# In every slot, TensorE projects the values' columns before it transposes the attention's outputs, instead of after

## The reference

```
q, k, v = split(shift_tokens(x) @ Wqkv[i])           # 16 heads of 64
q, k    = rotary(l2norm(q) * q_scale), rotary(l2norm(k) * k_scale)
sim     = q @ k_window.T * 8, masked                  # windows of 32 tokens, each looks at itself and the one before
x       = softmax(sim) @ v_window  merged @ Wo + x
a, gate = split(layernorm(shift_tokens(x)) @ W1 + b1)
x       = a * gelu(gate) @ W2 + b2 + x
```

## Time and profile before

| | |
|---|---|
| time, median of 3 runs | 4077.79 us (4077.22 to 4078.13) |
| the profiled execution: its own time | 4067.75 us |
| its span, first to last instruction | 4066.0 us |
| granted TensorE clock, mean over the span | 0.964 of 2.4 GHz |
| PE busy | 3616.5 us, 89% of the span |
| weight loads (overlap PE) | 2665.1 us, 66% |
| DVE busy | 2853.2 us, 70% |
| ACT busy | 2465.4 us, 61% |
| POOL busy | 1858.0 us, 46% |

### The profile page before, as it was taken

How to read it: one execution, slowest core, us unless ns; L and a number is a source line. 1 busy time by engine, 2 the same in 40 slices (tenths; PEclk the granted TensorE clock), 3 DMA queues, 4 the chain that set the end, 5 groups by cost and what they waited for, 6 DMA issues and landing times. The chain is left out here.

```text
span 4066.0 us, 155656 instructions
## 1 busy us (share of the span) xinstructions
PE 3616.5 (89%) x66756; PEld 2665.1 (66%) x66756; DVE 2853.2 (70%) x4768; ACT 2465.4 (61%) x4661; POOL 1858.0 (46%) x1559
## 2 busy tenths in 40 slices
PE   4996998998999998999998999998999998999995
PEld 3884666666666666666666666666666666666663
DVE  3116777778777778777778777777777777777773
ACT  2224666667666666666666666666666666666664
POOL 2003554455545555555545544544544545445441
PEclk9667999999999999999999999999999999999998
DMA  2211101111101011110111100111100111101002
GB/s 51 41 20 48 34 27 29 32 44 39 32 27 33 28 49 36 30 32 27 33 44 36 34 28 27 33 44 36 34 28 27 33 44 36 34 28 32 28 28 73
DMA packets 163065, 142.00 MB, mean 35 GB/s; under 512 B 87097, under 2 KB 112464, under 8 KB 161616
## 3 DMA queue, kind: packets, MB, share of 16 engines
q1 hardware_dynamic: 155866, 132.04, 11.9%
q10 hardware_dynamic: 6518, 0.03, 0.1%
HBM read 28.35 MB, written 6.36 MB: 9 GB/s over the span
## 5 line engine op out<-in xcount | busy, mean ns | idle before, releaser
L1094 POOL TENSOR_TENSOR nat<-ra,rb 128x512 f32<-128x512 f32 x768 | 1003.0, 1306 | 1154.4 <-DVE ra L1149 1137.8
L1098 POOL TENSOR_TENSOR nat<-nat,rr 128x512 f32<-128x512 f32 x768 | 820.1, 1068 | 675.8 <-ACT rr L1048 620.7
L1148 DVE TENSOR_TENSOR rb<-ps,tab 128x512 f32<-128x512 f32 x768 | 526.3, 685 | 342.8 <-ACT sq L988 340.1
L785 PE MATMUL ps<-wh,xls 128*128 128x512 f32 x1152 | 613.9, 533 | 29.7 <-PEq L132 29.6
L988 ACT ACTIVATE sq<-ps 128x512 f32<-128x512 f32 x768 | 449.4, 598 | 190.6 <-PE ps L787 146.9
L820 PE MATMUL ps<-kT,qT 64*32 64x64 f32 x24704 | 450.4, 220 | 94.3 <-issue 91.6
L1149 DVE TENSOR_TENSOR ra<-ps,tab 128x512 f32<-128x512 f32 x768 | 522.4, 680 | 0.0
L820 PEld LDWEIGHTS ps<-kT,qT 64*32 64x32 f32 x24704 | 372.0, 106 | 193.0 <-issue 177.4
L801 PE MATMUL ps<-con,nat 128*128 128x128 f32 x3080 | 425.7, 274 | 47.7 <-POOL nat L1098 37.7
L1180 DVE TENSOR_REDUCE nrm<-sq 128x16 f32<-128x1024 f32 x384 | 463.8, 1208 | 0.0
L786 PE MATMUL ps<-wl,xhs 128*128 128x512 f32 x1152 | 458.5, 398 | 0.0
(11 more groups left out here) (165 smaller groups left out, 5710.1 us busy)
## 6 DMA issues: line engine op xcount, KB each, us to landing
v<-v SPq DMA_DIRECT2D x192, 396.0 KB, 3.6
v<-v SPq DMA_DIRECT2D x96, 132.0 KB, 3.5
raw<-in_L_ffn_Wqkv SPq DMA_DIRECT2D x6, 1536.0 KB, 6.5
v<-v SPq DMA_DIRECT2D x96, 66.0 KB, 3.2
vbd<-vD SPq DMA_DIRECT2D x128, 32.2 KB
wo<-in_L_ffn_Wo SPq DMA_DIRECT2D x6, 512.0 KB, 5.2
xnat<-in_L_attn_hidden_states SPq DMA_DIRECT2D x8, 256.0 KB, 3.5
vD<-vs SPq DMA_DIRECT2D x8, 256.0 KB, 2.3
```

Source lines behind the costliest of these rows:

```text
L785: nc.tensor.matmul(dst, al, bh, start=True, stop=False)
L1094: nc.gpsimd.tensor_tensor(nat[:, k, :], ra[:, k, :], rb[:, k, :], ALU.add).then_inc(cur["add"], 1)
L1098: nc.gpsimd.tensor_tensor(nk, nk, rr[:, k, :].unsqueeze(2).broadcast_to([P, 8, DH]), ALU.mult).then_inc(cur["qkn"], 1)
L1148: nc.vector.tensor_tensor(heads8(rb[:, k, :]), heads8(ps[:, bank, :])[:, :, ::-1, :], sin, ALU.mult)
```

## The change

In PE's list of a slot, the wait for `ke` and `project(i, 2, TT)` move from behind the previous row's piece to between `scores` and `turn_out`. Nothing is added or removed, and the lists of the other engines are the same.

```diff
@@ def tensor(pe), the loop over the slots
                     scores(i)
+                if full:
+                    pe.wait_ge(cur["ke"], i + 1)
+                    project(i, 2, TT, cur["v"])
                 if live(i, 3):
                     turn_out(i)
                 if i == 0:
...
                 if i == 2:
                     pe.wait_ge(cur["otev"], 2)
                     out_proj(4)
-                if full:
-                    pe.wait_ge(cur["ke"], i + 1)
-                    project(i, 2, TT, cur["v"])
                 if i == 1:
                     out_proj(2)
```

## The result

The changed kernel takes 4104.99 us (median of 5 runs, 4096.22 to 4109.73) against 4077.22 us before (median of 5 too, 4066.06 to 4078.13): ratio 1.007, 95% interval 1.0055 to 1.0085. That is 28 us, 0.58 us a round, where 36 us and 0.75 were forecast. The profiled execution took 4109.73 us, at the slow end of its runs, and that of the kernel before 4067.75, at the fast end of its own; the traces show how things moved, and the sizes have to come from the timed runs.

The account below looks back on a forecast made before the run. PE was taken to bound the kernel, busy 89% of the span, with waits for DVE's `on` and ACT's exponential. Slot terms sum to 0.75 us a round, x 48 = 36 us, giving 4114 us; range 4076 to 4142.

Parts of the forecast that it names:

- How late `turn_out` gets: Behind `scores` and the moved projection, `turn_out` starts 0.71 us after the scores' end; lower bound 0.55, upper bound 1.00.
- The exponential 1.89 after the scores: On ACT, the exponential follows the copy `oT`, so starts no earlier than 1.18 us after `turn_out`, 1.89 after the scores' end.
- Slot 3: +0.50: The mean follows `turn_out` 0.50 us late, and `fc`, the square, the variance and slot 4's start move with it.
- Slot 7: +0.30: Exponential and `turn_probs` start later, 0.23 us normally and 0.41 where scores are held up; 0.30 on average.
- Slot 6: +0.10: `up` waits for ACT's copy of the values: 0.25 us later where held up, otherwise nothing; 0.10 on average.
- Slots 4 and 5: 0: PE's gain of about 0.2 us in slot 4 only lengthens slot 5's wait for ACT's exponential; sum 0.
- the fourth rival: Slower by more, through PE's clock or the upper bound; one more clock fall in half the rounds, 4152 us; chance 0.10.
- Slots 0 and 1: 0: Two `out_proj` matmuls cover the chain; PE gains up to 0.2 us, but the next `turn_projection` waits for POOL's k.
- Slot 2: -0.15: Four `out_proj` matmuls cover the chain, so the 0.16 us a round waited before `turn_out` is won.
- The held-up scores as they were: Scores that stop halfway with no engine to wait for, 91.6 us in total, were expected unchanged in number.
- Rival 1: Faster: the wait before `turn_out` is filled and nothing replaces it; at most 86.5 us back, 3991 us; chance 0.12.
- Rival 2: No difference: the group behind `scores` delays `turn_out` by 0.4 us or less; slot 2 gives back slot 3's loss, 4078; chance 0.13.

Follow-up runs that it names:

- the early mean: Slot 3 alone moved, mean's matmul put ahead of `turn_out`, ACT's order exponential, `fq`, `oT`, against the kernel before: 4075.02 against 4077.62 us, ratio 0.9993.

## Why the prediction was right, and where it was off

The sign, the range and the main step hold: PE lost what lay between `turn_out` and `turn_probs` to fill its time, and the wait moved behind ACT's order. That the size fits is in part luck, as its terms show. Step by step:

- **How late `turn_out` gets:** 0.71 forecast, 0.72 to 0.74 measured. The price taken from the nearest row was right: the trace shows 0.80 from the projection's start to `turn_out`'s. The estimate of 0.31, by the spacing of 131 ns that the Trainium skill gives (TensorE: Matmul & The Clock Gate, Back-to-back issue gap), did not come true.
- **The exponential 1.89 after the scores:** 1.84 in slot 3, 1.86 in slot 7.
- **Slot 3: +0.50:** 0.48 undisturbed. Timed alone 16 us, 0.34 a round (0.20 to 0.47). Right in mechanism, as the changed kernel's slot 3 and the early mean show; a third too large in time.
- **Slot 7: +0.30:** 0.19 undisturbed against 0.23, 9.43 against 9.06 where held up (0.37 against 0.41), so the chain is right. As a term of the time it was mis-sized: 2 us timed alone, 0.05 a round (at most 0.15). Some 5 us come back in slot 0's held-up scores; the rest is open.
- **Slot 6: +0.10:** held up 0.22 longer, where 0.25 was forecast; undisturbed 0.08 shorter, where nothing was. That is 0.04 a round. Timed alone it is 1 us (-4 to 7), none that can be told.
- **Slots 4 and 5: 0:** right for the undisturbed slots (-0.17 and +0.15), wrong as a term. Slot 5 costs 9 us and slot 4 saves 6, both without a change in the two slots' sum, and both with the clock. The wait of 0.85 was read in a held-up slot; in the others it was 0.41 and 1.54, and a wait of 1.98 took their place. This is the fourth rival's mechanism, which had 0.10 with half a fall more a round. By the mean clock it is an estimated 9 us of the 28, so it was part of the likeliest case and not another one.
- **Slots 0 and 1: 0:** right undisturbed: from k to k 8.38 and 8.97 before and after. The next `turn_projection` follows POOL's k by 0.15.
- **Slot 2: -0.15:** wrong in size. The waits counted there were those of 11 rounds. Nine of these slots, undisturbed in both traces, are 0.5 to 0.7 shorter, so the wait was won there. The others are mostly a little longer, the median is 10.69 against 10.66, and the mean over the 43 undisturbed in both is 0.06 less. Slot 2 wasn't tried alone. Slots 0 to 2 together cost 9 us when timed, 7 of them by the estimate from the clock.
- **The held-up scores as they were:** not quite. Their total is 83.1 instead of 91.6 us in the profiled execution. With slot 5's move there are 13 or 14 of them in slots 6 and in slots 7 instead of 18. Two of those in slot 4 are over 3 us.

So the forecast 36 against 28 comes from terms that were too large (slots 3, 6 and 7, together about 24 us too much by the single moves), and from what wasn't in the sum: slots 4 and 5 with 4 us, and slots 0 to 2 with 9 us lost where 7 were to be gained (together about 19). The sum was closer than its parts, and that is luck. The range's upper end of 4142 is not the 4162 that the upper bound gave, and no step of the prediction leads to it.

Rival 1, the wait simply filled, fell: outside nine slots 2, the waits that were saved come back before `turn_probs` (slot 4's in slot 5) or behind POOL's k (slots 0 and 1). Rival 2 fell with the measured 0.80.

## What to carry to other kernels

Before filling a gap in an engine's list, ask what stood behind the gap and what the moved work had covered: here the same 0.8 us covered a copy and an exponential on ACT, and moving it cost more than the gap was worth. On the other engine, put what is ready first in front; that alone (slot 5's exponential ahead of a copy) gave 7 us, about as much as the move gave in the one slot where it paid (slot 4, 6 us). Read a wait in a typical slot, not in a held-up one. And count idle time of PE by its pieces as well as by its sum: here one wait of 1.98 us cost clock where 0.41 and 1.54 apart didn't.

## What the runs showed of the hardware that was not expected

The granted clock follows not only how much PE idles but how its idle time is cut. With the same undisturbed slot lengths, joining slot 5's idle into one wait of 1.98 us took the mean clock from 0.9616 to 0.9564, with 12 of 19 falls in that slot. Filling slot 4's gap of 0.92 us, which left less idle time in that slot, raised it to 0.9631. Executions of one and the same kernel differ by up to 28 us, the kernel before from 4064 to 4092, and 0.6 of the variance goes with the mean clock.

Scores that are held up with no engine to wait for are held until a point in time, it seems, more than for a length of time: with slot 5 shorter by 0.49 the stand in slot 6 grew from 0.39 to 0.53 a round, and with slot 7 longer by 0.19 that in slot 0 shrank from 0.57 to 0.46. Each is from one profiled execution. The trace before has something at that point in time. Ahead of each of its 97 stands of over 0.3 us a packet of 16 KB starts on the instruction queue (q8), 0.8 to 1.9 us before the stand begins, and the stand ends 2.2 to 2.8 us after that packet's start. The two long stands of the changed kernel end 2.5 and 2.2 us after such a start too, but there the packet starts 0.9 us after the stand has begun. This would fit a wait for the next instructions. It isn't shown: 120 of the 287 slots that aren't held up have such a packet close ahead of their scores too, and no run varies where the code lies.
